# A gated recurrent layer on TensorE: the output projection y put between update gate and candidate, x pieces moved behind it

## The reference

```python
def step(H, xs):
    xz, xr, xh = xs                       # x @ W.T + b of every step
    Z = jax.nn.sigmoid(xz + H @ Whz.T + bhz)
    R = jax.nn.sigmoid(xr + H @ Whr.T + bhr)
    H_tilda = jnp.tanh(xh + R * H @ Whh.T + bhh)     # (R * H) @ Whh.T
    H_new = Z * H + (1.0 - Z) * H_tilda
    Y = H_new @ Whq.T + bhq
    return (H_new, Y)
return x + transpose(Y of all steps)
```

## Time and profile before

| | |
|---|---|
| median of three runs | 524.96 us |
| profiled execution | 523.88 us |
| its span, first to last instruction | 522.0 us |
| TensorE matmul busy | 510.2 us, 98% |
| weight loads busy | 492.3 us, 94% |
| VectorE busy | 317.6 us, 61% |
| ScalarE busy | 329.2 us, 63% |
| granted TensorE clock, mean | 1.000 |
| HBM traffic | 53 GB/s over the span |

### The profile page before, as it was taken

One profiled execution on the slowest core, in us unless ns is written; L12 is line 12 of the kernel. 1 busy time (PEld: TensorE's weight loads), 2 busy tenths in 40 slices (PEclk: granted clock), 3 DMA queues, 4 the chain that ended last, 5 costly groups with the idle time before them and its releaser, 6 DMA issues.

```text
span 522.0 us, 96066 instructions
## 1 busy us (share of the span) xinstructions
PE 510.2 (98%) x44184; PEld 492.3 (94%) x44184; DVE 317.6 (61%) x1929; ACT 329.2 (63%) x1800; POOL 0.2 (0%) x4
## 2 busy tenths in 40 slices
PE   8499999999999999999999999999999999999997
PEld 7499999999999999999999999999999999999997
DVE  1266666666666666666666666666666666666665
ACT  2266666666666666666666666666666666666665
POOL 0000000000000000000000000000000000000000
PEclk9999999999999999999999999999999999999999
DMA  5111121111111111111221111111111111111111
GB/s 176 29 51 45 50 55 46 50 55 45 51 55 45 51 54 45 52 54 45 53 53 45 55 51 45 54 51 45 55 50 45 55 51 45 55 50 45 55 50 51
DMA packets 57735, 27.63 MB, mean 53 GB/s; under 512 B 6784, under 2 KB 56832, under 8 KB 57728
## 3 DMA queue, kind: packets, MB, share of 16 engines
q1 hardware_dynamic: 56880, 26.70, 18.4%
q10 hardware_dynamic: 848, 0.83, 0.5%
HBM read 18.98 MB, written 8.52 MB: 53 GB/s over the span
## 4 chain that ended last, share of the span: by engine, by line
PE 96%; issue 2%; DMA 1%; SPq 0%; DVE 0%; ACT 0%; ACTq 0%; DVEq 0%
PE r_ps L244 34%; PE c_ps L244 28%; PE z_ps L244 23%; PE y_ps L244 11%; DMA whq_sb<-in_whq_dram 1%; SPq L114 0%; SPq L115 0%; SPq L116 0%; SPq L112 0%; DVE u_sb L230 0%; DVE o_sb L212 0%; DVE h_sb L235 0%; ACT c_sb L189 0%; DVE rh_sb L225 0%; ACT r_sb L179 0%
## 5 line engine op out<-in xcount | busy, mean ns | idle before, releaser
L244 PE MATMUL c_ps<-xt_sb,wx_sb 128*32 128x64 f32 (+1 forms) x4104 | 172.8, 225 | 1.5 <-issue 1.5
L244 PE MATMUL z_ps<-xt_sb,wx_sb 128*32 128x64 f32 (+1 forms) x4104 | 163.3, 220 | 0.0
L179 ACT ACTIVATE r_sb<-r_ps 128x32 f32<-128x32 f32 x512 | 91.3, 198 | 106.1 <-PE r_ps L244 98.7
L225 DVE TENSOR_TENSOR rh_sb<-r_sb,h_sb 128x32 f32<-128x32 f32 x512 | 89.8, 192 | 85.3 <-ACT r_sb L179 81.1
L244 PE MATMUL z_ps<-h_sb,whz_sb 128*32 128x32 f32 x8192 | 123.9, 198 | 2.2 <-issue 2.2
L244 PE MATMUL c_ps<-rh_sb,whh_sb 128*32 128x32 f32 x8192 | 122.6, 198 | 2.2 <-issue 1.9
L244 PE MATMUL y_ps<-whq_sb,h_sb 128*32 128x128 f32 x2064 | 113.5, 279 | 0.3 <-DVE h_sb L235 0.3
L244 PEld LDWEIGHTS z_ps<-h_sb,whz_sb 128*32 128x32 f32 x8192 | 108.7, 110 | 2.4 <-issue 2.4
L244 PE MATMUL r_ps<-xt_sb,wx_sb 128*32 128x64 f32 (+1 forms) x4104 | 108.2, 219 | 0.0
L230 DVE SCALAR_TENSOR_TENSOR u_sb<-z_sb,c_sb 128x32 f32<-128x32 f32 x512 | 75.2, 188 | 53.5 <-ACT c_sb L189 53.5
L244 PEld LDWEIGHTS z_ps<-xt_sb,wx_sb 128*32 128x32 f32 (+1 forms) x4104 | 101.1, 110 | 0.0
(11 more groups left out here) (27 smaller groups left out, 359.3 us busy)
## 6 DMA issues: line engine op xcount, KB each, us to landing
xt_sb<-in_xt_dram SPq DMA_DIRECT2D x130, 64.0 KB, 1.8
xres_sb<-in_xr_dram SPq DMA_DIRECT2D x130, 64.0 KB, 1.8
out_dram<-o_sb SPq DMA_DIRECT2D x130, 64.0 KB, 1.6
wx_sb<-in_wx_dram SPq DMA_DIRECT2D x3, 256.0 KB, 3.4
whr_sb<-in_whr_dram ACTq DMA_DIRECT2D x1, 256.0 KB, 5.0
whz_sb<-in_whz_dram ACTq DMA_DIRECT2D x1, 256.0 KB, 5.1
whh_sb<-in_whh_dram ACTq DMA_DIRECT2D x1, 256.0 KB, 5.6
whq_sb<-in_whq_dram SPq DMA_DIRECT2D x1, 256.0 KB, 6.4
```

Of the source, the lines that this page charges most:

```text
L179: nc.scalar.activation(r_sb[:, o], r_ps[:, o, here], ACT.Sigmoid).then_inc(s_r[o], 1)
L225: nc.vector.tensor_tensor(rh_sb[:, k], r_sb[:, k], old[:, k], ALU.mult).then_inc(s_rh[k], 1)
L244: return nc.tensor.matmul(ps, weights, moving, start=start, stop=False, skip_group_check=True, **kw)
```

## The change

Only the order of TensorE's instructions changes. In the steps u = 0, 1, 2 the y part (4 matmuls of 128 columns) stands directly behind z, the first Z piece moves from in front of c to behind it, and the second R piece moves behind the zh parts, where y stood. In step u = 3 the order stays as it was. The waits move with their instructions: that for y's seed with y, that for Z's seed in front of the Z pieces behind c. `s_xt_used` is still fired by the last R piece of the steps with s = 1, which in u = 1 now stands behind the zh parts.

```diff
--- before.py
+++ after.py
@@ -265,6 +265,13 @@
                     last = mm(y_ps[p][B * j:B * j + B, 0, 0:P], h_sb[:, k, CS * p + step], whq_sb[:, k, P * half:P * half + P],
                               tile_position=(0, B * j))
                 return last
+
+            def y_step(t, q, s):
+                if s == 0:
+                    pe.wait_ge(s_seed_y, t + 1)
+                last = y_piece(q, s)
+                if s == CS - 1:
+                    last.then_inc(s_y_ps, 1)
 
             def r_part(u, k, o, moving):
                 return columns(r_ps[:, o], slice(B * u, B * u + B), whr_sb, k, o, moving)
@@ -337,10 +344,12 @@
                         for k in range(K):
                             z_mm = columns(z_ps[p][:, 0], slice(W * o + B * s, W * o + B * s + B), whz_sb, k, o, old[:, k])
                     z_mm.then_inc(s_z_ps, 1)
+
+                    if u < SLOTS - 1:
+                        y_step(t, q, s)
                     x_piece(q, N, pieces[1])
-                    if s == 0:
-                        pe.wait_ge(s_seed_z, t + 1)
-                    x_piece(q, Z, pieces[0])
+                    if u == SLOTS - 1:
+                        x_piece(q, Z, pieces[0])
 
                     for k in range(K):
                         pe.wait_ge(s_rh[k], t + 1)
@@ -349,21 +358,25 @@
                             if k == K - 1:
                                 c_mm.then_inc(s_c_ps[o], 1)
 
+                    if s == 0:
+                        pe.wait_ge(s_seed_z, t + 1)
+                    if u < SLOTS - 1:
+                        x_piece(q, Z, pieces[0])
                     x_piece(q, Z, pieces[1])
                     if s == 0:
                         pe.wait_ge(s_seed_r, t + 1)
-                    for piece in pieces:
-                        x_mm = x_piece(q, R, piece)
-                    if s == CS - 1:
-                        x_mm.then_inc(s_xt_used, 1)
+                    x_mm = x_piece(q, R, pieces[0])
+                    if u == SLOTS - 1:
+                        x_mm = x_piece(q, R, pieces[1])
                     pe.wait_ge(s_zh, t + 1)
                     for k, o in AHEAD[(u + 1) % SLOTS]:
                         r_part((u + 1) % SLOTS, k, o, zh_sb[:, k])
-                    if s == 0:
-                        pe.wait_ge(s_seed_y, t + 1)
-                    y_mm = y_piece(q, s)
+                    if u < SLOTS - 1:
+                        x_mm = x_piece(q, R, pieces[1])
+                    else:
+                        y_step(t, q, s)
                     if s == CS - 1:
-                        y_mm.then_inc(s_y_ps, 1)
+                        x_mm.then_inc(s_xt_used, 1)
 
             pe.wait_ge(s_seed_y, T + 1)
             for k in range(K):
```

## The result

The changed kernel takes **531.98 us** (median of four runs, 530.34 to 532.28) where the kernel before, run beside it, takes 525.34: the ratio is 1.0116, with a 95% interval of 1.0095 to 1.0137. It is slower, by 6.6 us. The forecast had +3.2 us: the sign was right and the size was about half of what came.

What follows compares the result with a forecast made beforehand. TensorE was taken as nearly back to back, with waits for rh before c and u after. Intervals of +0.02, 0, -0.08 and +0.11 gave +0.05 us an iteration, times 64 +3.2 us: 528.2 us, range 522 to 534.

Steps and rivals of the forecast that it cites:

- c no longer stops for rh: Inside c, steps 0 to 2: both halves of rh are there in time, so c takes 0.27 us instead of 0.29.
- tanh comes sooner: Behind c: tanh starts 0.45 to 0.46 us after c's start instead of 0.48, 0.02 to 0.03 earlier.
- second rival: Behind c: tanh stays at 0.48, every wait is paid, c to c 1.98 to 1.99 us; 534 us, chance 0.24.
- Free restarts: r's 24 records behind u's second half: resuming after a wait costs nothing, 0.18 us; the forecast took 0.03 a stop.
- first rival: r behind u's second half: restarts cost nothing, c to c 1.91 us instead of 1.95; 521.8 us, chance 0.15.
- The boundary grows: Interval from step 3 to the next step 0: +0.11 us, from the work added in front of c.
- the interval 2 to 3 shrinks: c of step 2 to c of step 3, no y in front: 1.84 to 1.85 us for 1.92, -0.08.
- the boundary's side behind c: Step 3 to next step 0, behind c: unchanged, because TensorE waits there for u anyway.
- The value for c to c: Steps 0 to 1 and 1 to 2: terms summed from c's start give 1.95 to 1.96 us, taken as 1.95.
- third wait of r: r's late part: h's first half reaches TensorE 1.14 to 1.15 us after c's start, wanted after 16 more records.
- third rival: Around c: time saved on rh equals the new wait for u; within 1 us of before; 0.61 together with the forecast.

Runs made afterwards that it cites:

- e10: The changed kernel with the new order in step 0 alone, the other steps as in the kernel before: 528.08 us, ratio 1.0052.
- e6: The changed kernel with r's late parts reading zh, not u and h, and the u wait only before r's last part; different results: 522.63 us, ratio 0.9958.
- e11: The changed kernel with the new order in all four steps, step 3 included: 536.31 us, ratio 1.0209.
- e8: The kernel before with one R piece (0.11 us) moved from step 2 into step 3: 528.27 us, ratio 1.0075.
- e7: The kernel before with 32 of the second Z piece's 64 columns moved in front of c in steps 0 to 2: 526.32 us, ratio 1.0034.
- e4: The changed kernel with the second R piece back in front of r's zh part: 532.43 us, ratio 1.0150.
- e2: The changed kernel with only two of y's four matmuls before c, two last, and the first Z piece behind c, steps 0 to 2: 559.49 us, ratio 1.0653.
- e5: The changed kernel with r's late parts reading zh in steps 1 to 3 and the u wait behind r, before N; different results: 537.90 us, ratio 1.0242.
- e12: The kernel before with TensorE's loop unrolled twice, 32 passes of eight steps: 1419.25 us, ratio 2.7034.

## Why the prediction was right in sign and too small

**c no longer stops for rh: right.** 0.27 was forecast, and from c's start to the next group it is 0.25. In e10's rows c has 0.45 with x30 in the changed step and 0.48 with x32 in the others. **tanh comes sooner: right**, and this is what refutes the second rival's mechanism: tanh starts 0.451 us behind c (0.475 before), and u's halves are usable at 0.926 and 1.028, where the forecast had 0.93 and 1.02. The second rival's 534 is nearer to the result than the forecast's 528.2, and its mark for a loss of over 1%, c to c above about 1.96, was met by 1.966; but tanh did not stay at 0.48, and the 1.98 to 1.99 that it built on this did not come.

**Free restarts: wrong, as forecast.** The first rival needed c to c under 1.93. With the stops it is 1.966, and without them 1.915 (e6): the restart and the stop are paid, 0.051 us of the interval. The restart alone can be read from r's 24 records behind the wait for u's second half: 0.212 us, where zh's 24 take 0.187 in the same steps. That is 0.025, for the 0.03 that the forecast had.

**The boundary grows, the interval 2 to 3 shrinks: right.** +0.104 and -0.068 for +0.11 and -0.08. The reason given for the boundary's side behind c, that TensorE waits there for u anyway, was wrong: it waits for the end of the loop body (e11, e8). The number came out because the change leaves that end where it was, 0.731 us behind c for 0.727.

**The value for c to c: the step that failed.** The sum ended in "the next c starts at 1.95 to 1.96. I take 1.95", and measured is 1.966. The working, term by term, from the start of c:

| us behind the start of c | forecast | measured |
|---|---|---|
| u usable, first and second half | 0.93, 1.02 | 0.926, 1.028 |
| r ends (start of the first N piece) | 1.23 | 1.240 |
| that N piece, width | 0.12 | 0.115 |
| z, width | 0.27 | 0.275 |
| y, width | 0.22 | 0.226 |
| second N piece, width | 0.11 to 0.12 | 0.112 |
| next c | 1.95 | 1.966 |

The mechanism held, and its terms were mis-sized. None is off by more than 0.010 us, but nearly all are off to the same side, and three times the lower of two values was taken: 1.02 of 1.02 and 1.03 for u's second half, 0.22 for a y that the earlier trace rows show with 0.23, and 1.95 of 1.95 and 1.96 at the end. A third wait of r, for h's first half, was put at nothing, as h was reckoned there when wanted (1.14 to 1.15). Its load comes at 1.152, 0.053 us behind VectorE's end and 0.017 behind the load before it, where the others of that part follow at 0.006 to 0.010; what that costs lies inside r's last 24 records, 0.212 us for the forecast's 0.21. So three intervals were 0.015 us too short each; less 0.007 too much at the boundary that makes 0.04 us an iteration, 2.4 us over the loop. The forecast change was a difference of two sums of some 7.8 us that came out at 0.05; at such a ratio an error of 0.5% in the sum is nearly the whole answer.

**What the sum left out.** It counted the loop alone. Between the medians about 1 us more lies outside the steady iterations (6.6 less 5.6). In the profiled pair that is the first iteration, 1.17 us longer because its instructions arrive at other places in the order. Single executions of the other kernels end it anywhere from 26.09 (e7) to 27.95 us (e4), and the trace has no rule in it for which order does well.

**The third rival, slack only shifts,** holds for a shift of half the size (e7: +0.013 us an iteration). It was right about the kind of curve and wrong about where on it this change lies.

## What to carry to other kernels

Where an engine is nearly back to back between two waits of a loop of dependence, count the slack on both sides before work is moved from one side to the other: up to that slack the move costs nothing and gains nothing, beyond it every nanosecond taken away turns into a stop, and the side that receives it pays in full. Such slack (0.05 to 0.09 us here) is not in busy times nor in the list of waits; it is read as the distance from the load that was waited for to its matmul (84 ns before, 2 ns after). Idle time of an engine at a loop's end is slack only if its queue is not busy with the branch: here 0.11 us put there cost 0.08 (e8). And where a forecast is a small difference of long sums that repeats 64 times, take the terms in nanoseconds over many iterations, and take the middle of each.

## What the runs showed of the hardware

- Where TensorE waits for VectorE inside the loop body, the waiting load starts 53 ns behind the end of the producer (u's first half, steps 0 to 2, before and after alike).
- The loop's end costs TensorE time of its own: the branch stands in its queue for 208 ns, and the first load of the next iteration comes 359 ns behind the branch's start, whether u was ready 35 ns before (before) or 140 ns before (e8).
- Four matmuls on the four quarters of the array cost as much as two of them: two quarters of y take the 0.22 us of the whole (e2).
- Two waits in a row ahead of one group become a load with a wait and an instruction of 51 ns of its own; both were already satisfied, and the loads on either side stand 138 ns apart, for 15 ns with one wait (e5, e6).
- A loop body of eight steps does not stay with TensorE, one of four does: 2.7 times the time (e12).
- In the first iteration TensorE stops four times for 1.4 to 2.5 us to get instructions. Behind that the granted clock was at its lower level in the profiled execution of the changed kernel and not in that of before. In 35 of 54 executions of the kernel before the mean clock is under 0.999, and they take 1.2 us more; where in the span they lose it, only a profile would show.
